# The fourth fc2 tile of a slot in front of the transposes of h, in a two-layer recurrent and feed-forward kernel

## The reference

```python
# layer 1, on the layer-normalised x; then x = x + this
pre = x @ W + b                               # 256 -> 1024, split into i, f, o, z
i = 10 * tanh((i_pre + input_bias) / 10); f = -softplus(f_pre)
o = sigmoid(o_pre);                       tz = tanh(z)
# scan over the steps
m_next = maximum(f + m, i)
c = exp(f + m - m_next) * c + exp(i - m_next) * tz
n = exp(f + m - m_next) * n + exp(i - m_next)
h = o * (c / (n + 1e-6))
out = h / sqrt(mean(h * h) + 1e-8) * scale
# layer 2; then x = x + this
r = layernorm(x)
y = silu((layernorm(r) * gamma + beta) @ w1 + fc1_bias)   # 256 -> 1024
out = r + 0.5 * (y @ w2 + fc2_bias)                       # 1024 -> 256
# w1 and w2 are dequantised: (q - 128) * scale
```

## Time and profile before

| | |
|---|---|
| median of 3 runs | 367.61 us (367.4 to 368.43) |
| span of the profiled execution | 363.6 us |
| its own time | not listed apart; the median is 4.0 us more than the span |
| PE matmul busy | 318.1 us, 87% |
| DVE busy | 284.5 us, 78% |
| POOL busy | 220.3 us, 61% |
| ACT busy | 195.5 us, 54% |
| mean granted TensorE clock | 0.962 |

### The profile page before, as it was taken

One profiled execution on the slowest core, in us unless ns is written; L12 is line 12 of the kernel. 1 busy time (PEld: TensorE's weight loads), 2 busy tenths in 40 slices (PEclk: granted clock), 3 DMA queues, 4 the chain that ended last, 5 costly groups with the idle time before them and its releaser, 6 DMA issues.

```text
span 363.6 us, 5243 instructions
## 1 busy us (share of the span) xinstructions
PE 318.1 (87%) x1760; PEld 272.1 (75%) x1760; DVE 284.5 (78%) x482; ACT 195.5 (54%) x309; POOL 220.3 (61%) x176
## 2 busy tenths in 40 slices
PE   0768949997989979998999979998869988999995
PEld 0657737777868978787878978788747777799795
DVE  2796939997859798697959798597997998776841
ACT  1573925764447833774456833775475830960820
POOL 1293895897279933997279933997279934512500
PEclk9999989999999989999899989999996989899999
DMA  6982000000050001400050000400030000300101
GB/s 196 395 304 59 1 0 1 2 1 0 2 173 3 0 2 34 140 2 0 1 171 2 0 0 22 152 0 0 2 115 0 0 2 0 115 3 2 59 0 58
DMA packets 15155, 18.34 MB, mean 50 GB/s; under 512 B 800, under 2 KB 14368, under 8 KB 14880
## 3 DMA queue, kind: packets, MB, share of 16 engines
q1 hardware_dynamic: 14704, 17.83, 14.7%
q10 hardware_dynamic: 432, 0.27, 0.5%
HBM read 13.90 MB, written 4.19 MB: 50 GB/s over the span
## 4 chain that ended last, share of the span: by engine, by line
POOL 37%; DVE 24%; issue 21%; PE 12%; ACT 3%; DMA 2%; POOLq 1%; SPq 0%; DVEq 0%; ACTq 0%
POOL xn L874 7%; POOL base L874 5%; POOL rec L894 4%; POOL rrms L904 3%; DVE bn L613 3%; POOL g L874 3%; POOL r L880 3%; POOL base L929 3%; POOL r L911 2%; POOL rec L900 2%; DVE y_lo L737 2%; PE mm_ps L319 2%; PE mm_ps L320 2%; PE mm_ps L321 2%; DVE rec L656 2%
## 5 line engine op out<-in xcount | busy, mean ns | idle before, releaser
L319 PE MATMUL z_ps<-w_hi,y_hi 128*128 128x256 f32 x256 | 76.0, 297 | 2.3 <-DVE y_lo L737 2.3
L321 PE MATMUL z_ps<-w_hi,y_lo 128*128 128x256 f32 x256 | 73.6, 287 | 0.0
L320 PE MATMUL z_ps<-w_lo,y_hi 128*128 128x256 f32 x256 | 73.5, 287 | 0.0
L540 ACT ACTIVATE y<-mm_ps,b_all 128x512 f32<-128x512 f32 x64 | 42.9, 683 | 20.8 <-DVE y_lo L737 13.6
L319 PEld LDWEIGHTS z_ps<-w_hi,y_hi 128*128 128x128 f32 x256 | 50.1, 196 | 4.7 <-DVE y_lo L737 4.4
L320 PEld LDWEIGHTS z_ps<-w_lo,y_hi 128*128 128x128 f32 x256 | 50.2, 196 | 0.3
L737 DVE TENSOR_TENSOR y_lo<-y,y_hi 128x512 fp32r<-128x512 f32 x64 | 47.2, 764 | 3.7 <-ACT y_hi L544 2.6
L321 PEld LDWEIGHTS z_ps<-w_hi,y_lo 128*128 128x128 f32 x256 | 49.7, 194 | 0.0
L319 PE MATMUL mm_ps<-xt_hi,wg_hi 128*128 128x512 f32 x112 | 46.6, 416 | 0.5 <-ACT rec L509 0.5
L321 PE MATMUL mm_ps<-xt_hi,wg_lo 128*128 128x512 f32 x112 | 45.3, 405 | 0.0
L320 PE MATMUL mm_ps<-xt_lo,wg_hi 128*128 128x512 f32 x112 | 45.3, 404 | 0.0
(11 more groups left out here) (111 smaller groups left out, 707.8 us busy)
## 6 DMA issues: line engine op xcount, KB each, us to landing
base<-x SPq DMA_DIRECT2D x8, 512.0 KB, 4.3
out<-out_sb SPq DMA_DIRECT2D x16, 256.0 KB, 2.3
x_in<-x SPq DMA_DIRECT2D x7, 512.0 KB, 4.8
q<-fc_q SPq DMA_DIRECT2D x2, 1024.0 KB, 12.4
wg_raw<-w_gates SPq DMA_DIRECT2D x2, 512.0 KB, 8.4
s<-fc_scales SPq DMA_DIRECT2D x1, 1024.0 KB, 12.0
wg_raw<-fc_scales SPq DMA_DIRECT2D x1, 1024.0 KB, 9.5
x_in<-x SPq DMA_DIRECT2D x2, 256.0 KB, 4.3
```

The source lines that it names most:

```text
L319: pe.matmul(dst, wh[w_at], ah[a_at], start=first, stop=False)
L320: pe.matmul(dst, wh[w_at], al[a_at], start=False, stop=False)
L321: return pe.matmul(dst, wl[w_at], ah[a_at], start=False, stop=last)
L540: act.activation(y[:, j % 3], mm_ps[:, j % 4], ACT.Silu, bias=b1_all[:, j:j + 1]).then_inc(silu_done, 1)
```

## The change

In slots 2 to 6 the fourth fc2 tile is issued before the transposes of h, and no longer after them. Nothing is added or removed, and the other engines' programs are the same.

```diff
@@ -466,9 +466,9 @@
                 if nxt.exists:
                     x_turned(nxt)
                 fc2(ffn, 2)
+                fc2(ffn, 3)
                 if mixed.exists and not early_h(t):
                     h_turned(mixed)
-                fc2(ffn, 3)
```

## The result

The changed kernel takes 378.22 us (median of 4 runs, 376.58 to 379.81), the kernel before 367.65 (4 runs, 367.4 to 368.43). The ratio is 1.0285, with a 95% interval of 1.0242 to 1.0327: slower by 10.6 us, where 4.95 had been forecast and 375.5 was the end of the range. The direction was right, and the forecast size was less than half of the measured one.

What follows compares the result with a forecast made beforehand. The prediction took a ring of POOL and DVE work as the bound, passing to PE. It added 0.47 (slot 2) and 4.48 (1.12 per slot, slots 3 to 6) to 367.61, giving 372.6 us, range 368.0 to 375.5.

Steps and rivals of the forecast that it cites:

- What bounds the kernel, and that the order by itself is free in slots 3 to 6: A ring of POOL and DVE work sets the period; the swap by itself costs 0.0 per slot in slots 3 to 6.
- Slot 2's 0.47: In slot 2 the later transposes of h move the mean square from 94.27 to 94.74, +0.47 us, once.
- The wait for g: The 3.9 us that PE wins stand as one wait ahead of the transposes of g.
- The clock falls behind it in each of slots 3 to 6: PE's granted clock falls behind the new wait for g in each of slots 3 to 6, as in slot 7.
- The price of a fall, 1.33 us of PE: Each clock fall behind the wait for g costs PE 1.33 us, with 0 and 2.53 kept for the range.
- the 1.12 of the forecast: The mean square comes at 218.49, 1.12 us behind today's 217.37: +1.12 per slot over slots 3 to 6, +4.48.
- the long drop: Rival, chance 0.09: each wait for g brings slot 7's loss of 2.53, a slot costs 2.32, time 377.4 us.
- Whether the loss lands: PE's loss at the transposes of g reaches h in full, less 0.14 us for the y_lo wait in fc2 tile 0.
- the last one (DVE's h later by more than 1.2 us): Sign of being wrong: DVE's h over 1.2 us later would mean that the reciprocal carries the loss.
- The price by the rule of half the throttled time: The skill's rule prices a clock drop as half the throttled time: 1.54 us, an estimate, giving 373.4 for the sum.
- The sum: Slot 2's 0.47 and 4.48 over slots 3 to 6 make +4.95 us, for a time of 372.6 us.
- The base: The median stands 4.0 us above the profiled span of 363.6; the sum was added to the median, 367.61.

Runs made afterwards that it cites:

- e1: The changed kernel with 14 matmuls whose results nobody reads ahead of the transposes of g in slots 3 to 6; 367.53 us against 367.16, ratio 1.0008.
- e4: The kernel before with fc2 tile 3 moved ahead of the transposes of h in slot 2 alone; 370.57 us against 367.16, ratio 1.0109.
- e10: The kernel before with 14 matmuls whose results nobody reads ahead of the transposes of g in slot 7 only; 367.18 us against 366.73, ratio 1.0007.
- e3: The changed kernel with POOL's product o*c started only after DVE's last y_lo of the slot; 375.53 us against 367.16, ratio 1.0227.
- e5: The changed kernel with POOL's o*c held until the last y_lo and its b2 addition until DVE's denominator; 375.01 us against 367.55, ratio 1.0216.
- e7: The changed kernel with POOL's i*z started only after DVE's three steps of h; 377.51 us against 367.55, ratio 1.0264.
- e9: The kernel before with POOL's i*z only after h, and unread matmuls ahead of g's transposes (9 in slots 3 to 6, 14 in slot 7); 363.12 us, ratio 0.9893.
- e8: The kernel before with 12 of fc2 tile 3's 24 matmuls moved ahead of the transposes of h; 368.97 us against 367.55, ratio 1.0017.
- e6: The kernel before with POOL's i*z started only after DVE's three steps of h, slots 2 to 6; 367.87 us against 367.55, no interval.

## Why the prediction was right in its side and wrong in its size

*What bounds the kernel, and that the order by itself is free in slots 3 to 6*: right. Slot 5 of the change and e1 show it, with 41.08 and 41.02 us against 41.0 to 41.1. Slot 2's 0.47 was somewhat too large: in e1 and e4, with this order and the clock up, the mean square of slot 2 stands 29.92 us behind the transposes of g against 29.63, so 0.3. The lengths of slot 2 don't measure it: e10, with the order of before, has 42.15 us like e1.

*The wait for g*: right, 3.74 to 4.00 us against 3.9.

*The clock falls behind it in each of slots 3 to 6*: nearly. It fell in three of four in the profile of the change, and in all four in those of e3, e5 and e7. The reason given, that the wait is as long as slot 7's, isn't enough, as slot 5 shows.

*The price of a fall, 1.33 us of PE*: right for one form only. A short fall with the collisions gone costs 1.05 to 1.2 us per slot (e3's slot 5, e5's slots 4 and 6), which is the 1.12 of the forecast. But the fall of slot 6 was a long one and cost 2.23, close to the 2.32 of the rival "the long drop", which the range left out, and e3 and e5 had one or two such falls too. I had called the long drop of slot 7 a matter of slot 7.

*"Whether the loss lands"*: this is the step that failed. It counted PE's lateness as passing to h one for one, less a wait for `y_lo` that would vanish. In its place that wait grew from 0.14 to 1.68 us, since a late fc1 makes DVE's last `y_lo` miss its turn before POOL's product, and POOL starts that product 0.77 us earlier. A slot with a short fall then costs 3.03 to 3.06 us, of which some 2.0 is the collision (3.05 less the 1.05 of e3, a difference of slots from two profiles). If the fall takes the transposes of g, `gt_lo` is late by 0.7 and the carry copy collides with POOL's addition, worth 1.0 (e3's 2.1 and 2.2 against e5's 1.1 and 1.2). The prediction had the row that warned: h's second step at 3.30 us beside i*z. It read that as a property of that one place, and not as something that awaits each DVE instruction that comes late.

Of the prediction's own signs of being wrong, the last one (DVE's h later by more than 1.2 us) shows in slot 6 only: `xt_lo` starts 27.30 us behind the transposes of g there, 25.08 before, behind a reciprocal that is 2.2 us late. In slots 3 and 4 it is 0.16 us late, as the prediction had argued, and the lateness is all PE's.

The Trainium skill, page "SBUF — State Buffer", section "SBUF: two separate sides", says that DVE and GpSimd share a pair of ports under an exclusive lock, which whoever starts first keeps for its whole instruction; on DVE's side it concerns instructions in a two-port mode, and those with two inputs in SBUF when the GpSimd one reads SBUF. The rows of slot 3 agree: POOL starts at 127.72, DVE at 128.07, and DVE ends 0.56 us after POOL, a little under the 0.69 to 0.77 that a `y_lo` takes otherwise. So does the copy in e3's slot 4, which had been issued 1.02 us after POOL's addition and ends 0.02 after it. What the runs show is that the order of the two decides; that the cause is a port is the page's word and no run here separates it.

*The price by the rule of half the throttled time*: the Trainium skill, page "TensorE: Matmul & The Clock Gate", section "HAM oscillation — how this bites in real kernels". In slot 6 the clock is 0.50 over all 4.5 us, so a loss of 2.25 over that stretch by the rule, an estimate; the slot cost 2.23. The agreement is rough: the clock stayed down a little beyond the stretch (0.58 from 244.6 to 245.6). For the short falls the rule gives 4.5 x (1 - 0.625) = 1.7, an estimate, where the slots without a collision cost 1.05 to 1.2.

*The sum*: 0.77 + 3.06 + 3.03 - 0.05 + 2.23 = 9.04 us between the transposes of g of slots 2 and 7, against 0.47 + 4.48. By slots the forecast was short by 0.30 in slot 2 and by 1.94 and 1.91 in slots 3 and 4, which is the failed step; slot 5, spared, gave 1.17 back and slot 6, with its long fall, took 1.11, and that these two cancel is luck. The medians differ by 10.6, and the 1.5 us between that and 9.04 are not traced. Four runs of the change lie in two pairs, at 376.6 and 376.9 and at 379.5 and 379.8, with mean granted clocks of 0.950 in the first and 0.941 and 0.932 in the second; that the pairs differ in the number and form of their falls is likely and wasn't shown.

*The base*: the prediction took the median as 4.0 us above the span. In the later runs 1.7 to 3.0 us lie around the span, 1.8 in most. The term cancels out, as the sum was added to the median.

What stays open: why the same wait of 3.74 us left the clock up in slot 5 and not in slot 3. No experiment varied it.

## What to carry to other kernels

Before moving work into an engine's wait, ask where the wait will stand afterwards: one that lay behind other work and cost nothing (ahead of the transposes of h) was moved to a place from which the whole next slot hangs, and took a fall of TensorE's clock with it. A fall of the clock there must be priced twice, as PE's own loss, and as lateness of what follows, up to the next place where a late DVE instruction falls behind a long POOL one that it used to precede. The second price can't be read off PE's slack at one wait: in e4 PE still had 2.14 us of it, and the slot was 2.19 us longer. If a wait can't be removed, filling it with matmuls that nobody reads is a cheap test of the clock's part, and with 9 of them in slots 3 to 6, 14 in slot 7 and one POOL instruction held back it gave a kernel 1.1% faster than the one before (e9).

## What the runs showed of the hardware that had not been expected

A fall of the clock behind a wait isn't a matter of the wait's length alone: behind 3.74 us it stayed at 1.00 in slot 5 of the change and fell in its slot 3, behind 2.57 to 2.67 us (e8) it stayed in four of four, in e6 it fell behind 2.48 and 2.62 us and stayed behind 2.61, and behind 2.37 us ahead of the transposes of h it fell in slots 4 and 5 of before. And its effect comes in forms, short (0.62 to 0.63 over 4.5 us) and long (0.50).

A DVE copy of 128x6 elements was held for 2.19 us by a POOL addition on other tensors: the size of the delayed instruction says nothing of what a collision costs.
